# First attention stage in four pipeline steps, its normalisations on ScalarE

## What is computed

```python
q = ln(x) @ w_q.T;  k = ctx @ w_k.T;  v = ctx @ w_v.T
x = x + tanh(g_xattn[0]) * softmax(q @ k.T / sqrt(128)) @ v     # per batch entry
h = ln(x)
logits = h @ Wg                                                  # 8 experts, top 2
x = x + tanh(g_ffn[0]) * sum_e score_e * (relu(h @ W1_e + b1_e) @ W2_e + b2_e)
# then 16-head masked attention and a sigmoid-routed gated MLP with a shared expert
```

## Time and profile before

| | us |
|---|---|
| median of 3 runs | 767.61 (767.25 to 768.88) |
| the profiled execution's own time | 765.61 |
| its span | 763.8 |
| PE busy in the span | 653.7 |
| DVE busy | 566.9 |
| ACT busy | 427.8 |
| POOL busy | 94.4 |

### The profile page before, as it was taken

The page is one execution under the profiler, slowest core; times in us unless marked ns, Lnnn a source line. Parts: engine busy times, 40 slices in busy tenths (PEclk is TensorE's granted clock), DMA queues, the critical chain, the costliest instruction groups (busy, mean ns, idle before and its releaser), DMA issues.

```text
span 763.8 us, 12816 instructions
## 1 busy us (share of the span) xinstructions
PE 653.7 (86%) x4094; PEld 504.1 (66%) x4094; DVE 566.9 (74%) x1275; ACT 427.8 (56%) x665; POOL 94.4 (12%) x125
## 2 busy tenths in 40 slices
PE   5686665799999999994798988988988379999996
PEld 4574443687778778773576766766765258888884
DVE  3767576888889889887577766866865678888885
ACT  3243221577777777772376666665765045555553
POOL 3344230200000000003001011011001100000000
PEclk9657665899999999998599999999999589999998
DMA  5322000000000000003233313413400000000000
GB/s 160 101 81 82 27 8 0 1 1 0 1 0 0 0 0 0 0 1 98 61 101 102 104 41 95 113 35 90 111 2 1 0 1 0 15 14 14 27 14 28
DMA packets 23698, 29.24 MB, mean 38 GB/s; under 512 B 3313, under 2 KB 17522, under 8 KB 23666
## 3 DMA queue, kind: packets, MB, share of 16 engines
q1 hardware_dynamic: 23666, 28.84, 13.3%
HBM read 19.99 MB, written 8.85 MB: 38 GB/s over the span
## 4 chain that ended last, share of the span: by engine, by line
PE 67%; DVE 18%; issue 5%; POOL 5%; ACT 4%; DVEq 1%; DMA 0%; SPq 0%; ACTq 0%; POOLq 0%
PE psum L371 12%; PE psum L373 12%; PE psum L372 12%; PE psum L1160 5%; PE psum L1175 3%; PE psum L1150 2%; DVE xn L300 2%; DVE stats L281 2%; POOL rstd L293 2%; PE psum L1151 2%; PE psum L360 2%; PE psum L1466 2%; PE psum L858 2%; PE psum L319 1%; DVE a_rg L632 1%
## 5 line engine op out<-in xcount | busy, mean ns | idle before, releaser
L1270 ACT ACTIVATE c_pt<-psum 77x512 f32<-77x512 f32 x128 | 74.6, 586 | 57.4 <-PE psum L1160 57.3
L371 PE MATMUL psum<-xh,w_hi 128*128 (+1 forms) x248 | 102.0, 411 | 2.6 <-DVE d_hr L1554 2.6
L372 PE MATMUL psum<-xl,w_hi 128*128 (+1 forms) x248 | 99.1, 400 | 0.0
L373 PE MATMUL psum<-xh,w_lo 128*128 (+1 forms) x248 | 98.9, 399 | 0.0
L813 DVE TENSOR_TENSOR b_hl<-b_hs,b_hh 128x1024 fp32r<-128x1024 f32 x64 | 78.2, 1222 | 18.0 <-ACT b_hh L807 17.9
L916 ACT ACTIVATE b_hr<-psum,b1s 128x512 f32<-128x512 f32 x128 | 81.1, 686 | 16.8 <-PE psum L373 16.8
L958 DVE TENSOR_TENSOR b_hs<-b_hr,psum 128x1024 f32<-128x1024 f32 x64 | 78.8, 1231 | 12.7 <-ACT b_hr L916 11.5
L807 ACT ACTIVATE b_hh<-b_hs 128x1024 fp32r<-128x1024 f32 x64 | 67.9, 1061 | 34.3 <-PE psum L373 34.1
L1160 PE MATMUL psum<-ident,c_pf 128*77 128x128 f32 x512 | 74.7, 283 | 0.0
L1160 PEld LDWEIGHTS psum<-ident,c_pf 128*77 128x77 f32 x512 | 58.3, 149 | 14.3 <-issue 9.6
L1330 DVE TENSOR_REDUCE c_mx<-psum 128x8 f32<-128x616 f32 x64 | 51.0, 796 | 21.6 <-PE psum L1151 21.0
(11 more groups left out here) (206 smaller groups left out, 1328.0 us busy)
## 6 DMA issues: line engine op xcount, KB each, us to landing
w_hi<-c_q_spread SPq DMA_DIRECT2D x24, 256.0 KB
stage<-in_weights SPq DMA_DIRECT2D x8, 576.0 KB, 4.2
c_q_spread<-w_hi SPq DMA_DIRECT2D x8, 512.0 KB, 3.4
ctxg<-in_ctxT SPq DMA_DIRECT2D x16, 156.0 KB, 4.3
c_k_spread<-w_lo SPq DMA_DIRECT2D x8, 312.0 KB, 2.2
x_all<-in_x SPq DMA_DIRECT2D x8, 256.0 KB, 3.0
out_dram<-x_all SPq DMA_DIRECT2D x8, 256.0 KB, 2.3
c_kb<-c_k_spread SPq DMA_DIRECT2D x48, 39.0 KB
```

The costliest lines, as they stand in the source:

```text
L371: pe.matmul(o, wh, h, start=start, stop=False)
L372: pe.matmul(o, wh, l, start=False, stop=False)
L373: return pe.matmul(o, wl, h, start=False, stop=stop)
L1270: a_.activation(pt[:, q % NC4, :], bank[2 + q % 2][0:S2, :], ACT.Copy).then_inc(pt_done, 1)
```

## The change

- `pipeline4` takes the place of `pipeline` in stage `a`. A step has four groups: `a`, `m`, `t` and `u`, each one behind the other. There are eleven steps: four at the start, four in the loop, three at the end. The logits of a group (three products, copy, transposes, copy) belong to `u`, one step later than before.
- `dve_norm` is no longer called in this stage. GpSimd computes `-mean * rstd` in two more instructions of 128x4 (`pool_shift`), and ScalarE computes xn as `Identity(rstd * x + shift)` in four activations of 128x128 (`act_norm`), both for `ln0` (group `a`) and `ln1` (group `t`).
- GpSimd: rstd and shift of `a` come first, then those of `t`, then the low part of the weights.
- TensorE's order in a step: scores of `m`, logits product of `u`, transposes of `a`, keys and values of `a`, logits transposes of `u`, transposes of `t`, transposed probabilities and output product of `m`. Before: scores of `m`, keys and values of `a`, transposed probabilities of `m`, transposes of `t`, output product of `m`, transposes of `a`, logits of `t`.
- ScalarE's order: norm of `a`, logits copy of `u`, copy of the transposes of `a`, exp of `m`, norm of `t`, copies of keys and values of `a`, high part of `t`, copy of the transposed probabilities of `m`, split of the weights.
- VectorE's order: statistics of `a`, residual and statistics of `t`, maximum and shift of `m`, logits copy of `u`, sums of `m`, low part of `t`.
- The transposed logits go to bank 7 (where the products were) and no longer to bank 6. SP's part is unchanged.

In the diff the bodies of `scores`, `keys_values`, `probs`, `outs`, `residual`, `shift` and `sums` are left out: they are the old statements under a name.

```diff
...
+def pipeline4(eng, step):
+
+    def groups(i, c):
+        return [Group(i, c - k) if c - k >= 0 and (i is not None or c - k < NG) else None for k in range(4)]
+    for c in range(4):
+        step(*groups(None, c))
+    with eng.Fori(0, (NG - 4) // 2) as i:
+        step(*groups(i, 4))
+        step(*groups(i, 5))
+    for c in range(NG, NG + 3):
+        step(*groups(None, c))
...
+            def pool_shift(self, q, g, nm):
+                _, m, _, rs, _ = self.bufs
+                p = g.parity
+                q.tensor_scalar(nm[:, p, :], m[:, p, :, 0], -1.0, None, ALU.mult).then_inc(self.centred, 1)
+                q.wait_ge(self.rstd_ready, g.at(1, 1))
+                q.wait_ge(self.centred, g.at(1, 1))
+                q.tensor_tensor(nm[:, p, :], nm[:, p, :], rs[:, p, :], ALU.mult).then_inc(self.moved, 1)
+
+            def act_norm(self, a, g, nm):
+                _, _, _, rs, xo = self.bufs
+                p = g.parity
+                a.wait_ge(self.moved, g.at(1, 1))
+                for t in range(TG):
+                    ins = a.activation(xo[:, p, t, :].rearrange("p (a c) -> p a c", a=1), x_all[:, g.tile(t), :], ACT.Identity,
+                                       bias=nm[:, p, t:t + 1], scale=rs[:, p, t:t + 1])
+                ins.then_inc(self.xn_ready, 1)
...
-        lg0 = RouterLogits("a_router", ln1, wg0h, wg0l, bank[7], bank[6])
+        lg0 = RouterLogits("a_router", ln1, wg0h, wg0l, bank[7], bank[7])
+        nm0, nm1 = sb("a_nm0", [P, 2, TG]), sb("a_nm1", [P, 2, TG])
...
         def pool_a(q):
-            def step(a, m, t):
+            def step(a, m, t, u):
+                if a:
+                    ln0.pool_rstd(q, a)
+                    ln0.pool_shift(q, a, nm0)
                 if t:
                     ln1.pool_rstd(q, t)
+                    ln1.pool_shift(q, t, nm1)
                 if a:
-                    ln0.pool_rstd(q, a)
                     pool_split(q, a)
-            pipeline(q, step)
+            pipeline4(q, step)
         pool_parts.append(pool_a)
 
         def pe_a(pe):
-            def step(a, m, t):
+            def scores(m):
...
+            def step(a, m, t, u):
                 if m:
...
+                    scores(m)
+                if u:
+                    if u.i is None and u.c == 0:
+                        pe.wait_ge(s_split, 1)
+                    else:
+                        pe.wait_ge(lg0.lg_copied, u.at(1, 0))
+                    lg0.pe_product(pe, u)
                 if a:
...
+                    ln0.pe_transpose(pe, a)
+                    keys_values(a)
+                if u:
+                    lg0.pe_transpose(pe, u)
                 if t:
                     ln1.pe_transpose(pe, t)
                 if m:
...
+                    probs(m)
+                    outs(m)
+            pipeline4(pe, step)
+        pe_parts.append(pe_a)
+
+        def act_a(a_):
+            def step(a, m, t, u):
                 if a:
...
+                    ln0.act_norm(a_, a, nm0)
+                if u:
+                    lg0.act_copy(a_, u)
+                    if not t:
+                        Route(0, HEAD, rt_tail).act_ratio(a_)
                 if a:
...
+                    ln0.act_high(a_, a)
                 if m:
                     p = m.parity
                     a_.wait_ge(a_sub, m.at(1, 1))
                     a_.activation(A["pr"][:, p, :, :], A["sm"][:, p, :, :], ACT.Exp,
                                   bias=zero_col[:, 0:1], scale=float(D) ** -0.5).then_inc(a_exp, 1)
+                if t:
+                    ln1.act_norm(a_, t, nm1)
+                if a:
+                    a_.wait_ge(a_k_ready, a.at(1, 1))
+                    a_.activation(A["k0"][:, a.parity, :], bank[1][:, 0:GK], ACT.Copy).then_inc(a_k_done, 1)
+                    a_.wait_ge(a_v_ready, a.at(1, 1))
+                    a_.activation(A["v0"][:, a.parity, :], bank[2][0:S2, :], ACT.Copy).then_inc(a_v_done, 1)
+                if t:
+                    ln1.act_high(a_, t)
+                if m:
                     a_.wait_ge(a_pt_ready, m.at(1, 1))
...
+                    a_.activation(A["pt"][:, m.parity, :], bank[4][0:S2, :], ACT.Copy).then_inc(a_pt_done, 1)
                 if a:
                     act_split(a_, a)
-                if t:
-                    ln1.act_high(a_, t)
-                if a:
-                    ln0.act_high(a_, a)
-                if t:
-                    lg0.act_copy(a_, t)
-                    if not m:
-                        Route(0, HEAD, rt_tail).act_ratio(a_)
-            pipeline(a_, step)
+            pipeline4(a_, step)
...
+            def step(a, m, t, u):
                 if a:
                     wait_apart(v, s_x[a.parity], a.pair(16, 16))
                     ln0.dve_stats(v, a)
                 if t:
...
+                    residual(t)
+                    ln1.dve_stats(v, t)
                 if m:
...
+                    shift(m)
...
+                if u:
+                    lg0.dve_copy(v, u)
+                if t and not m:
+                    v.wait_ge(s_split, NG)
+                    v.wait_ge(s_small, 16 * len(small))
+                    v.wait_ge(lg0.lg_copied, NG - 1)
+                    route.first(v)
+                if m:
+                    sums(m)
                 if t:
                     ln1.dve_low(v, t)
                     if not m:
-                        route.weights(v)
-                    lg0.dve_copy(v, t)
-            pipeline(v, step)
+                        route.second(v)
+                if u and not t:
+                    route.weights(v)
+            pipeline4(v, step)
         dve_parts.append(dve_a)
```

More of the change, by code:

```diff
@@ L274, in __init__ @@
                 self.centred = sem(f"{name}_centred")
+                self.moved = sem(f"{name}_shift_ready")
             def dve_stats(self, v, g):
@@ L503, in pe_a @@
         def pe_a(pe):
-            def step(a, m, t):
-                if m:
[L506 to L514, removed]
-                if a:
[L516 to L535, removed]
@@ new lines, in scores @@
+            def scores(m):
+                p = m.parity
+                pe.wait_ge(ln0.hi_done, m.at(1, 1))
+                pe.wait_ge(a_k_done, m.at(1, 1))
+                if not (m.i is None and m.c == 0):
+                    pe.wait_ge(a_sub, m.at(1, 0))
+                for b in range(TG):
+                    ins = pe.matmul(bank[3][:, b * SK:(b + 1) * SK], A["xt"][:, p, b * P:(b + 1) * P],
+                                    A["k0"][:, p, b * SK:(b + 1) * SK], start=True, stop=True)
+                ins.then_inc(a_s_ready, 1)
@@ new lines, in keys_values @@
+            def keys_values(a):
+                p = a.parity
+                pe.wait_ge(a_ctx[p], a.pair(16, 16))
+                if not (a.i is None and a.c == 0):
+                    pe.wait_ge(a_k_done, a.at(1, 0))
+                    pe.wait_ge(a_v_done, a.at(1, 0))
+                pe.matmul(bank[1][:, 0:GK], w_m0[:], ctxg[:, p, :], start=True, stop=True).then_inc(a_k_ready, 1)
+                for b in range(TG):
+                    ins = pe.matmul(bank[2][0:S2, b * P:(b + 1) * P], ctxg[:, p, b * SK:b * SK + S2],
+                                    w_wv0[:], start=True, stop=True)
+                ins.then_inc(a_v_ready, 1)
@@ L587, in dve_a @@
             route = Route(0, HEAD, route_buffers(stage[:].rearrange("p a c -> p (a c)")))
[L589 to L607, removed]
-                    s = bank[3][:, 0:GK].rearrange("p (b k) -> p b k", b=TG)[:, :, 0:S2]
-                    link = Link(v, a_ch1, m, 1)
-                    link(v.tensor_reduce(A["mx"][:, p, :], s, AX.X, ALU.max))
-                    v.tensor_tensor(A["sm"][:, p, :, :], s,
-                                    A["mx"][:, p, :].unsqueeze(2).broadcast_to([P, TG, S2]), ALU.subtract).then_inc(a_sub, 1)
@@ new lines, in residual @@
+            def residual(t):
+                p = t.parity
+                v.wait_ge(a_o_ready, t.at(1, 1))
+                for b in range(TG):
+                    ins = v.scalar_tensor_tensor(
+                        out=x_all[:, t.tile(b), :], in0=bank[5][:, b * P:(b + 1) * P].rearrange("p (a c) -> p a c", a=1),
+                        scalar=A["rg"][:, p, b:b + 1], in1=x_all[:, t.tile(b), :], op0=ALU.mult, op1=ALU.add)
+                ins.then_inc(a_res, 1)
+                wait_apart(v, a_res, t.at(1, 1))
```

77 lines of the change are left out of this document (37 added, 40 removed).

## The result

| | before | after |
|---|---|---|
| median of 8 runs each, us | 767.83 (765.17 to 772.27) | 770.56 (769.31 to 772.51) |
| ratio, 95% interval | | 1.0038 (1.0022 to 1.0055) |
| profiled execution, us | 765.61 | 771.48 |
| its span, us | 763.8 | 769.6 |
| mark P in step 1, in step 7 | 16.88, 101.87 | 28.70, 112.07 |

The change is slower by 0.38%. The forecast had that direction, but its 780.0 us is 9.4 too high, and the time lies 0.4 us under the low end of its range. The mark P is now the end of L630.

A forecast was written before the change was run, and what follows sets the result against it. A chain across engines, none of them full, was taken to bound the first stage. Start 29.0, step 14.4, five of 15.2 and end 28.8 put the `ss` copy at 148.2, 12.4 later: 767.6 + 12.4 = 780.0 us, range 771 to 787.

The forecast's parts named there:

- mark P: End of ScalarE's copy of the transposed probabilities in each first-stage step; forecast 29.0 us in step 1, 119.4 in step 7.
- What leaves: First stage, per step: VectorE loses normalisations and two waits, leaving roughly 5.9 us of work in 13 or more.
- the mean step of before: First stage before the change: six steps from mark P of step 1 to step 7, 14.17 us each.
- The ring, part (c): First stage: loop of split, low part, rstd, shift, norm; ScalarE idle 5.2 us, normalising from 6.24 us after mark P.
- Part (a): ScalarE, first stage: four Identity activations take 1.6 us, against 0.8 at the lower bound.
- Part (b): GpSimd, first stage: two more 128x4 instructions behind each rstd, 0.6 us for each layer norm.
- Start and end: First stage: step 1's mark P at 29.0 us; from step 7's mark P to the `ss` copy 28.8 us.
- The full step: First stage, mark P to mark P: 13.4 us at full clock to 16.0 at half, taken as 15.2.
- dense part: TensorE's work in a first-stage step, from 7.95 us after mark P to the next; runs mostly at half clock.
- rival C: First stage: step 13.9 us because ScalarE's norms cost 0.8 and the clock returns early; 772 us, chance 0.13.
- Rivals A and B: First stage, TensorE: A, full clock throughout, 762.6 us, chance 0.07; B, half clock all the way, 785.9 us, chance 0.2.
- The rest as a block: Everything behind the first stage's `ss` copy is unedited, so it shifts whole, 12.4 us later.

The follow-up runs named there:

- first two experiments: Changed kernel with GpSimd's low part one step later: 750.46 us; changed kernel with ScalarE's weight split moved earlier, behind the logits copy: 751.08 us.
- the filled kernel: Changed kernel plus 40 unread TensorE transposes of the identity in each of steps 3 to 7: 767.76 us in one run.

## Why the prediction was right or wrong

**What leaves, and the mean step of before.** Right in what leaves (VectorE 5.93 us busy in the step, 5.9 forecast). But I read one form of the low part's collision, L632 at 2.13 us, and the 14.17 us is an average of unlike steps: in four of the six L632 is held up (1.87 to 2.41 us), in one nothing is (13.46 us, at a granted clock of 0.50), and in the longest, 16.40, it is the normalisation (3.41 us). The shortest, 10.24, has no logits yet. The sum needed only the average, so this cost nothing here.

**The ring, part (c): right, to a tenth.** GpSimd's low part first, ScalarE idle 5.22 us (5.2 forecast) with its releaser on GpSimd, the normalisation at P + 6.28 (6.24 forecast), TensorE's transposes at P + 7.99 (7.95). The first two experiments show that it is the cause.

**Part (a): right.** Four Identity activations took 1.65 us (1.6 forecast, bounds 0.8 and 1.6): the nearest row, L1254, was the right one to take. The prediction's estimate by the prices of the Trainium skill ("ScalarE: Activation LUTs", What ACT_TABLE_LOAD costs) was added up wrongly: 4 x (186 + 2 x 93 + 107) - 3 x 93 ns is an estimated 1.64 us, not 1.58. The trace agrees with it, at 1.65. **Part (b): right**, 0.68 us from the end of rstd (76.07) to the end of the shift (76.75), against 0.6. **VectorE: right**, waits of up to 7.9 us (over 4 forecast), and L666 at 0.23.

**Start and end: right, the start partly by luck.** P of step 1 at 28.70 (29.0). From P of step 7 to the `ss` copy 28.22 us (28.8). I took 29.0 as a mix of the two levels, but up to 27.2 us TensorE's groups took the lengths of the lower one (transposes 1.09 us, keys 1.25, values 1.91), for which I had 29.65; the overlap told below and a faster last group (0.86) took the 0.95 us off. The profile gives a granted clock of 1.00 from 11.5 to 28.7, which these lengths don't bear out.

**The full step: the term that failed.** 15.2 us forecast, 13.93 measured over five steps (42.42 to 112.07). That is 6.35 of the 7.9 us by which the `ss` copy came earlier than forecast (140.29 against 148.2); step 2 gives 0.7, start and end 0.9. Since the transposes started at the forecast place, the whole error lies behind them: 5.95 us where I took 7.25. It has two parts.

First, my bounds were too high. I added the busy times of neighbouring groups on TensorE back to back, but a group starts before its neighbour ends. Transposes, keys and values took 3.65 us at a clock of 0.50 (78.59 to 82.24), not 1.11 + 3.03 = 4.14. The rows had it: in the earlier trace rows L525 starts 1.12 us behind L523, whose busy time is 1.33, and in the earlier trace rows 0.57 behind a group of 0.73. I used that overlap inside keys and values, and not at their neighbours. A kernel of these experiments shows the spacing of three groups of four transposes at the lower clock:

```profile
76.35 1.06 PE L391 MATMUL psum<-ident,lt_s 128*128 128x128 f32 x4
...
77.21 1.00 PE L350 MATMUL psum<-ident,xn 128*128 128x128 f32 x4
...
78.05 0.60 PE L568 MATMUL psum<-ident,a_pr 128*77 128x128 f32 x4
```

It is 0.84 to 0.86 us (the low part late, step from P = 66.85), not 1.11. With the measured start of L391 (P + 11.64), two such spacings, 1.11, 0.1 and the copy of 0.58, a dense part wholly at 0.50 gives 15.1 us; one wholly at 1.00 is the 12.7 to 13.2 of the filled kernel. I had 16.0 and 13.4, and took 15.2, 0.69 of the way. The same choice between the right bounds is 14.4 to 14.5: 0.7 to 0.8 us of the error.

Second, the clock. I let the dense part run "mostly at half". It ran at 0.50 for 3.65 us and at 0.98 for the last 2.30, and this came back in each of the five full steps, with 0.80 to 1.00 behind the keys and values: the granted clock of these steps is 0.75 or 0.76. That is the other 0.5 to 0.6 us. No row of before had this rhythm, so I could have known only that both levels occur; rival C had the clock return early, with a chance of 0.13.

**Rival C's numbers came true, for half of its reason.** It gave a step of 13.9, P of step 7 at 112 and the `ss` copy at 140.3; measured were 13.90, 112.07 and 140.29. That is luck in part: it wanted the normalisations at 0.8 us, and they took 1.65. In its place stood the overlap, which no case of mine had. Its own end was 772, and 771 the end of my range; the overlap should have been looked for before the range was closed. Rivals A and B fell: the clock neither stayed at 1.0 nor at 0.5.

**The rest as a block: less exact than the sum.** The span grew by 5.8 us, 4.5 of it before the `ss` copy; the medians differ by 2.7. From the copy to the end of the span is 628.0 us before and 629.3 after, and 627.4 to 630.2 in the profiled executions of the other kernels, none of which edits that part. Before's profiled execution was 2.2 below its median, after's 0.9 above. By the 4.5 us of the `ss` copy the median would be 772.3; it is 770.6. Why the part behind the copy scatters by up to 3 us isn't settled, and these 1.7 us stay open with it.

## What to carry to other kernels

When work moves to another engine, follow its inputs through every queue once round: a new wait at the head of one queue and a long instruction ahead of its releaser in another make a ring, and the cure may be one line of order (770.6 to 750.5 us here). A long GpSimd instruction should lie where VectorE has no TENSOR_SCALAR on SBUF tiles to do, or what it would hold up should be on ScalarE; decide both together, since each alone lost 7 to 9 us. In a sum, take the distance from start to start of neighbouring groups from the rows, not their busy times.

## What the runs showed of the hardware

Two things I had not expected. GpSimd's pass over 128x1152 doesn't only hold up the short L632 but a normalisation too, for nearly its whole length (4.48 against 2.22 us, 3.53 and 3.41 against 1.12), and leaves ScalarE alone. Nor does it hold up all that VectorE does: in the change the residual beside it (72.16) takes 1.10 us, against 1.12, and the statistics beside it (73.30) take 0.29 and 0.66, as they do clear of it (84.91). Who starts first seems to decide, one instruction at a time: L637, begun 0.05 us ahead of the low part, took its 0.23 us, while the four normalisations at 86.55, the first of them begun 0.18 us ahead, took 3.41. And in the change the granted clock rose from 0.50 to 0.98 inside the dense part of the step shown, though in the earlier trace rows a step with TensorE busy for 12.89 of 14.70 us stayed at 0.50 throughout; what tells the two apart was not tried.
